# A decoder layer's quantized feed-forward: codes of x packed by the scalar engine and transposed by DMA instead of by TensorE, with the order of the down products changed

## What is computed

```
x = x + attention(layernorm(x))                 # 16 heads, window 128, 4 sinks
x = x + experts(layernorm(x), token ids, ctx)   # 4 experts, each token goes to one
x = x + ffn(layernorm(x))

def ffn(x):                                     # hidden size 2048
    h = silu(bit_linear(x, w_gate)) * bit_linear(x, w_up)
    h = ln_weight * h * rsqrt(mean(h * h) + 1e-6)
    return bit_linear(h, w_down)

def bit_linear(x, w):                           # activations to 8 bits per row, weights to -1, 0, 1
    s = 127 / clip(max(abs(x), axis=-1), 1e-5)
    q = clip(round(x * s), -128, 127) / s
    return q @ weight_quant(w).T
```

## Time and profile before

| | before |
|---|---|
| median of 3 runs | 798.23 us |
| lowest and highest | 793.23 and 798.83 us |
| the profiled execution's own time | 794.88 us |
| its span, from first to last instruction | 793.1 us |
| feed-forward, first gate product to the end | 588.5 to 793.1 us |
| mean granted TensorE clock | 0.987 of full speed |
| busy in the span | PE 92%, DVE 75%, ACT 60%, POOL 42% |

### The profile page before, as it was taken

How to read it: one execution, slowest core, us unless ns; L and a number is a source line. 1 busy time by engine, 2 the same in 40 slices (tenths; PEclk the granted TensorE clock), 3 DMA queues, 4 the chain that set the end, 5 groups by cost and what they waited for, 6 DMA issues and landing times. The chain is left out here.

```text
span 793.1 us, 14108 instructions
## 1 busy us (share of the span) xinstructions
PE 727.6 (92%) x5130; PEld 504.6 (64%) x5130; DVE 595.6 (75%) x1102; ACT 472.5 (60%) x1024; POOL 332.9 (42%) x330
## 2 busy tenths in 40 slices
PE   5988999999999999999987969999998989889894
PEld 4766777777777777777754658888873444334341
DVE  6886766886668856766676547788878999999972
ACT  4555766666667666766565224444447767766761
POOL 2011204213142134354374244445546667767661
PEclk9999999999999999999999989999999999999998
DMA  9300021304030331215330176555331223323231
GB/s 315 111 1 28 27 70 65 108 28 161 28 107 28 107 133 54 81 55 184 110 102 7 39 257 222 183 187 207 99 123 27 66 81 104 84 83 91 67 79 40
DMA packets 55218, 78.33 MB, mean 99 GB/s; under 512 B 36335, under 2 KB 38383, under 8 KB 53424
## 3 DMA queue, kind: packets, MB, share of 16 engines
q1 hardware_dynamic: 46336, 51.99, 20.7%
q0 software_dynamic: 8528, 24.93, 9.2%
q10 hardware_dynamic: 288, 0.52, 0.2%
HBM read 56.92 MB, written 17.59 MB: 94 GB/s over the span
## 5 line engine op out<-in xcount | busy, mean ns | idle before, releaser
L556 ACT ACTIVATE probs<-s_ps,neg_max 128x512 f32<-128x512 f32 (+2 forms) x256 | 152.5, 611 | 19.2 <-DVE neg_max L725 17.6
L725 DVE TENSOR_REDUCE neg_max<-s_ps 128x2 f32<-128x1024 f32 (+2 forms) x128 | 124.6, 1015 | 33.9 <-PE s_ps L963 33.4
L983 PE MATMUL pT_ps<-ident,probs 128*128 128x128 f32 x832 | 113.9, 277 | 11.0 <-DVE probs L746 9.7
L568 ACT ACTIVATE probs<-pT_ps 128x512 f32<-128x512 f32 x96 | 57.5, 599 | 98.6 <-PE pT_ps L983 97.7
L983 PEld LDWEIGHTS pT_ps<-ident,probs 128*128 128x128 f32 x832 | 92.6, 142 | 26.1 <-DVE probs L746 12.3
L746 DVE COPY probs<-pT_ps 128x512 f32<-128x512 f32 x112 | 76.7, 685 | 37.1 <-PE pT_ps L983 36.4
L1678 POOL TENSOR_TENSOR xg_own<-h,ln_w_sb 128x512 f32<-128x512 f32 x64 | 83.2, 1311 | 34.2 <-DVE h L1764 32.4
L896 PE MATMUL side_ps<-w_hi 128*128 128x512 f32 x172 | 71.1, 413 | 0.0
L420 POOL TENSOR_TENSOR aT_hi<-norm,one_col 128x512 fp32r<-128x512 f32 x15 | 15.6, 1042 | 125.6 <-DVE norm L737 87.4
L1867 PE MATMUL y_ps<-w_tern,hqT 128*128 128x512 bf16 x256 | 65.2, 379 | 2.8 <-DMA hqT<-hq 2.0
L896 PE MATMUL side_ps<-w_hi,w_lo 128*128 128x512 f32 x172 | 67.5, 392 | 0.0
(11 more groups left out here) (282 smaller groups left out, 1764.3 us busy)
## 6 DMA issues: line engine op xcount, KB each, us to landing
w_piece<-w_ffn SPq DMA_DIRECT2D x24, 512.0 KB
w_stage<-w_ffn SPq DMA_DIRECT2D x12, 1024.0 KB
xres<-x POOLq DMA_DIRECT2D x4, 1024.0 KB, 5.8
xn<-x SPq DMA_DIRECT2D x3, 1024.0 KB
x<-xres POOLq DMA_DIRECT2D x3, 1024.0 KB, 4.9
xn<-c SPq DMA_DIRECT2D x2, 1024.0 KB, 5.0
v_next<-c SPq DMA_DIRECT2D x2, 1024.0 KB, 7.8
xn<-x SPq DMA_DIRECT2D x4, 256.0 KB, 3.7
```

The source lines that it names most:

```text
L556: nc.scalar.activation(weights[qt][:, h, at:at + width(qt)], s_ps[:, h, 0:width(qt)], ACT.Exp, bias=neg_max[:, qt % 2, h:h + 1], accum_out ...
L568: nc.scalar.activation(out, turned_p, ACT.Identity).then_inc(slot_copied[0], 1)
L725: nc.vector.tensor_reduce(neg_max[:, qt % 2, 2 * s:2 * s + 2], s_ps[:, 2 * s:2 * s + 2, 0:width(qt)], AX.X, ALU.max, negate=True).then_inc ...
L983: last = nc.tensor.transpose(pT_ps[:, k % 2, h * P:h * P + P], weights[qt][:, h, a:z], ident[:])
```

## The change

- DVE no longer rounds x. ACT does, at the end of its tile behind gate 3, and then packs the codes of x to bf16 in a new tile `xq` (`quantize_x`, `pack_x`). SP issues a DMA transpose of them (`turn_x`). TensorE's transposes of x and ACT's copy out of PSUM are gone.
- The down products come one chunk later, one of them in the next tile; `y_of` stands behind hidden 0 of the next tile and is for tile t - 3; the store and the gather on POOL come one tile later.
- ACT does gate 2 ahead of both packings of h, not between them.
- DVE does hidden 1 ahead of the scale and the rounding of h, not behind them.
- `mean_of` is a tensor_scalar instead of a scalar_tensor_tensor.
- In the last expert tiles DVE does the clip ahead of the maximum of x; ACT rounds and packs x of tile 0 in the last but one expert tile and of tile 1 behind the last.
- `h_turned` is one semaphore for each half, so that the first two down quarters wait for the first half only.

```diff
+    def pack_x(self, act, t):
+        act.wait_ge(self.xq_ready, t + 1)
+        if t:
+            act.wait_ge(self.xqT_ready, t * 16)
+        self.nc.scalar.activation(self.xq[:], self.xq_code, ACT.Identity, bias=self.minus_offset[:]).then_inc(self.xq_packed, 1)
+
+    def turn_x(self, sp, t):
+        sp.wait_ge(self.xq_packed, t + 1)
+        self.nc.sync.dma_start_transpose(self.xqT[:, t % 2], self.xq[:]).then_inc(self.xqT_ready, 16)
...
-        self.nc.vector.scalar_tensor_tensor(self.mean_rstd[:, i:i + 1], self.bn_mv[:, i, 0:1], -1.0, self.rstd[:, i:i + 1],
-                                            ALU.mult, ALU.mult).then_inc(self.mean_ready, 1)
+        self.nc.vector.tensor_scalar(self.mean_rstd[:, i:i + 1], self.bn_mv[:, i, 0:1], self.rstd[:, i:i + 1], -1.0,
+                                     ALU.mult, ALU.mult).then_inc(self.mean_ready, 1)
...
-        self.nc.vector.tensor_scalar(self.xq_big[:], self.xn[:], self.x_inv[:], CODE, ALU.mult, ALU.add).then_inc(self.xq_ready, 1)
+        self.nc.scalar.activation(self.xq_big[:], self.xn[:], ACT.Identity, scale=self.x_inv[:], bias=self.code[:]).then_inc(self.xq_ready, 1)
...
@@ experts, scalar engine
-            if s == ROUTED_TILES - 1:
-                front.wait_scattered(act, 10)
-                act.wait_ge(front.consts, 4)
-                front.xqT_of(act, 0)
...
             if s == ROUTED_TILES - 2:
+                act.wait_ge(front.consts, 5)
+                front.wait_scattered(act, 9)
+                front.quantize_x(act, 0)
+                front.pack_x(act, 0)
                 front.normalize_x(act, 1)
+        front.quantize_x(act, 1)
+        front.pack_x(act, 1)
...
@@ feed-forward, SP
-        for t in range(TILES - 1):
-            turn(t)
+        front.turn_x(sp, 1)
+        for t in range(TILES):
+            if inside(t - 1):
+                turn(t - 1)
+            if inside(t + 2):
+                sp.wait_ge(up_summed, (t + 1) * FC)
+                front.turn_x(sp, t + 2)
...
@@ feed-forward, scalar engine
             gate_of(t, 1)
-            if inside(t + 1):
-                front.xqT_of(act, t + 1)
+            gate_of(t, 2)
             if inside(t - 1):
                 pack(t - 1, 0)
-            gate_of(t, 2)
             if inside(t - 1):
                 pack(t - 1, 1)
             gate_of(t, 3)
+            if inside(t + 2):
+                front.quantize_x(act, t + 2)
+                front.pack_x(act, t + 2)
             squares(t, 0)
...
@@ feed-forward, vector engine
+            if inside(t - LATE_DOWN - 1):
+                y_of(t - LATE_DOWN - 1)
             if inside(t - 1):
                 sum_squares(t - 1)
             if inside(t + 2):
                 front.top_of_x(dve, t + 2)
+            hidden(t, 1)
+            if inside(t + 2):
                 front.scale_x(dve, t + 2)
             if inside(t - 1):
                 scale_h(t - 1)
                 quantize_h(t - 1)
-            hidden(t, 1)
             hidden(t, 2)
-            if inside(t + 2):
-                front.quantize_x(dve, t + 2)
             if inside(t + 3):
                 front.stats_of(dve, t + 3)
                 front.variance_of(dve, t + 3)
             hidden(t, 3)
-            if inside(t - LATE_DOWN):
-                y_of(t - LATE_DOWN)
         last = TILES - 1
         top_of(last, 0)
+        y_of(last - LATE_DOWN)
         top_of(last, 1)
...
@@ feed-forward, TensorE
-                if c == 1 and t and inside(t + 1):
-                    front.transpose_x(pe, t + 1)
-                if inside(t - LATE_DOWN):
-                    down(t - LATE_DOWN, c)
+                quarter = (t - LATE_DOWN) * FC + c - 1
+                if quarter >= 0:
+                    down(quarter // FC, quarter % FC)
+        down(TILES - LATE_DOWN - 1, FC - 1)
```

More of the change, by code:

```diff
@@ L1137, in set_consts @@
         nc.gpsimd.memset(self.minus_offset[:], -CODE_ZERO).then_inc(self.consts, 1)
+        nc.gpsimd.memset(self.code[:], CODE).then_inc(self.consts, 1)
         nc.gpsimd.memset(self.ident[:], 0.0).then_inc(self.consts, 1)
-        pool.wait_ge(self.consts, 3)
+        pool.wait_ge(self.consts, 4)
         nc.gpsimd.affine_select(out=self.ident[:], in_=self.ident[:], compare_op=ALU.not_equal, fill=1.0, base=0,
@@ L1201, in scale_x @@
             dve.wait_ge(self.gu_ready, t)
+            dve.wait_ge(self.xq_ready, t)
         self.nc.vector.tensor_scalar(self.x_max127[:], self.x_max[:], Q_EPS, 1.0 / QMAX, ALU.max, ALU.mult).then_inc(self.xq_step, 1)
@@ L1204, in scale_x, with quantize_x @@
         self.nc.vector.reciprocal(self.x_inv[:], self.x_max127[:]).then_inc(self.xq_step, 1)
-    def quantize_x(self, dve, t):
-        dve.wait_ge(self.xq_step, (t + 1) * XQ_STEPS)
+    def quantize_x(self, act, t):
+        act.wait_ge(self.xq_step, (t + 1) * XQ_STEPS)
         if t:
-            dve.wait_ge(self.xq_transposed, t)
-        self.nc.vector.tensor_scalar(self.xq_big[:], self.xn[:], self.x_inv[:], CODE, ALU.mult, ALU.add).then_inc(self.xq_ready, 1)
[L1212 to L1218, removed]
+            act.wait_ge(self.xq_packed, t)
+        self.nc.scalar.activation(self.xq_big[:], self.xn[:], ACT.Identity, scale=self.x_inv[:], bias=self.code[:]).then_inc(self.xq_ready, 1)
 def expert_rows(sh, front):
@@ L1490, in vector_program @@
                 front.mean_of(dve, 1)
-            if s == last - 1:
+            if chunk_of(s) is not None:
+                clip(chunk_of(s))
+            if s == last - 2:
                 front.top_of_x(dve, 0)
                 front.scale_x(dve, 0)
[L1494 to L1498, removed]
         front.stats_of(dve, 2)
@@ L1549, in tensor_program @@
             if s == ROUTED_TILES - 1:
-                pe.wait_ge(front.consts, 4)
-                front.transpose_x(pe, 0)
+                pe.wait_ge(front.consts, 5)
             pe.wait_ge(a_ready, s + 1)
@@ L1618, in ffn_phase @@
     h_transposed, hqT_ready = sem("h_transposed"), sem("hqT_ready")
-    hq_packed, h_turned = sem("hq_packed"), sem("h_turned")
+    hq_packed, h_turned = sem("hq_packed"), [sem("h_turned0"), sem("h_turned1")]
     y_summed, y_ready = sem("y_summed"), sem("f_y_ready")
@@ L1637, in gate_up @@
         if c == 0:
-            pe.wait_ge(xqT_ready, t + 1)
+            pe.wait_ge(xqT_ready, (t + 1) * 16)
         if c >= 2 or inside(t - 1):
@@ L1648, in sync_program @@
     def sync_program(sp):
+        front.wait_scattered(sp, 10)
+        front.turn_x(sp, 0)
         sp.wait_ge(front.w_clipped, CHUNKS)
@@ L1658, in turn @@
                 sp.dma_start_transpose(hqT[:, t % 2, n * FK // HALVES:(n + 1) * FK // HALVES, :],
-                                       hq[:, n * HALF:n * HALF + HALF]).then_inc(h_turned, 16)
-        for t in range(TILES - 1):
-            turn(t)
+                                       hq[:, n * HALF:n * HALF + HALF]).then_inc(h_turned[n], 16)
+        front.turn_x(sp, 1)
[5 more added lines that the diff above has]
+                front.turn_x(sp, t + 2)
     def gpsimd_program(pool):
@@ L1699, in gpsimd_program @@
                 front.gu_scale_of(pool, t + 2)
-            if inside(t - LATE_DOWN):
-                store(t - LATE_DOWN)
-            if t >= LATE_DOWN + 1 and inside(t - LATE_DOWN - 1 + len(homes)):
-                front.gather(pool, t - LATE_DOWN - 1 + len(homes))
+            if inside(t - LATE_DOWN - 1):
+                store(t - LATE_DOWN - 1)
+            if t >= LATE_DOWN + 2 and inside(t - LATE_DOWN - 2 + len(homes)):
+                front.gather(pool, t - LATE_DOWN - 2 + len(homes))
         rms_of(TILES - 1)
-        for t in range(TILES - LATE_DOWN, TILES):
+        for t in range(TILES - LATE_DOWN - 1, TILES):
             store(t)
@@ L1719, in pack @@
             if inside(t - 1):
-                act.wait_ge(h_turned, t * HALVES * 16)
+                act.wait_ge(h_turned[n], t * 16)
             nc.scalar.activation(hq[:, cols], hq_code[:, cols], ACT.Identity, bias=minus_offset[:]).then_inc(hq_packed, 1)
@@ L1860, in down @@
             else:
-                pe.wait_ge(h_turned, (t + 1) * HALVES * 16)
+                pe.wait_ge(h_turned[g // HALVES], (t + 1) * 16)
             if g == 0 and inside(t - 1):
```

12 lines of the change are left out of this document (4 added, 8 removed).

## The result

| | before | after |
|---|---|---|
| median | 795.75 us (4 runs, 793.23 to 798.83) | 808.47 us (4 runs, 805.08 to 812.56) |
| profiled execution, its own time and span | 794.88, 793.1 us | 807.24, 805.5 us |
| mean granted TensorE clock | 0.987 | 0.982 |
| a feed-forward tile | 11.81 us | 12.48 us |

The ratio of the times is 1.0169, with a 95% interval of 1.0133 to 1.0204. The changed kernel is slower by 1.7%. I had said 804 us, 0.9% slower, and a tile of 12.34 us.

The account below looks back on a forecast made before the run. DVE was taken as fullest, but the new tile as bound by an ACT and DVE loop: 11.81 us plus 0.53 of POOL blocking. Terms - 0.9 + 1.7 + 5.9 + 0.2 = + 6.9 us; forecast 804 us, range 791 to 812.

Parts of the forecast that it names:

- same: Outcome for the whole kernel: a change within about 1%, 8 us; chance 0.52.
- slower: Outcome for the whole kernel: slower by more than about 1%, 8 us; chance 0.33.
- start, up to gate 3 of tile 0: Hand-over from the experts: first gate product no longer waits for TensorE's x transposes; 0.9 us less, bounds 0 and 1.3.
- tiles 3 to 13: Steady feed-forward tiles: 12.34 us each instead of 11.81, 5.9 us more over eleven.
- tiles 14 and 15: Last feed-forward tiles, without work for x: 11.06 and 10.3 us, together 0.2 us more.
- tail: From hidden 3 to the last store: the same up to 0.1 us.
- two squares of 1.05: ACT between gate 3 and gate 0: two squares of h, 1.05 us each, within the 4.11 us to gate 0.
- G + 4.05: When DVE alone would reach hidden 0, G being the start of gate 3; ACT puts it at G + 4.82.
- The lock: DVE's rounding of h held up by POOL's second weighting: first half 0.53 us late per tile, bounds 0 and 0.72.
- Rival A: Rounding not held up by POOL's weighting, or POOL misses it: tile 11.81 us, time unchanged, 795 to 798 us; chance 0.24.
- Rival C: TensorE's clock halves after its 2 us idle stretch: 2.7 us more a tile, 35 over 13; chance 0.09 with other slowdowns.
- 10.3 us of DVE work: DVE's tile without waits: 11.81 less 0.43 for rounding x, 0.60 for mean_of and 0.47 for gate 2.

Follow-up runs that it names:

- b3: Changed kernel with a separate output for each of the two squares of h, so the second needn't wait for the first; tile 12.27 us against 12.48.
- a1: Changed kernel with POOL's second weighting waiting until both halves of the rounding of h are done; median 801.65 us, ratio 1.0065 to the kernel before.
- a0: Changed kernel as it is, run again with the kernel before on another chip; ratio 1.0130, tiles of 12.48 us.
- d4: Changed kernel with second square behind gate 0, POOL's wait for both roundings, gate 3 ahead of the second packing, f_code 64 bytes wide; median 786.97 us.
- b4: Changed kernel with mean_of as a scalar_tensor_tensor again; one run 807.31 us, steady tile 12.48 us.
- b1: Changed kernel with second square of h behind gate 0 and POOL's second weighting behind both roundings; median 787.07 us, ratio 0.9893 to the kernel before.
- b5: Changed kernel with gate 2 between the two packings of h again; one run 813.9 us, tile 13.05 us.

## Why the prediction was right, and where its sum was off

The sign, the mechanism and the place are as forecast: ACT is what hidden 0 waits for, the rounding is held up by the weighting, and TensorE idles in one piece ahead of y_ps. The size is not. The measured median lies within the range, 4.5 us above the forecast and nearer to its edge than I should like. That the forecast came so near is luck in part: the 798.23 us that I built on came down to 795.75 with a fourth run, and from there the same sum gives 802.7. The 1.7% is beyond the 1% that I had allowed for "same", so of my three outcomes it is "slower", which had 0.33, and not the likelier "same". By spans the change is + 12.4 us, above even the + 3.5 to + 10.5 that I gave my own forecast, where the sum said + 6.9:

| term | forecast | measured |
|---|---|---|
| start, up to gate 3 of tile 0 | - 0.9 | + 1.2 |
| tiles 1 and 2 | + 1.7 | + 1.9 |
| tiles 3 to 13 | + 5.9 | + 7.7 |
| tiles 14 and 15 | + 0.2 | + 1.6 |
| tail | 0 | - 0.1 |

**The loop.** By the distances in the timeline after: gate 3 to gate 0 is 4.31 us (forecast 4.11), to hidden 0 0.70 (0.71), to the rounding 4.07 (4.1), to the packing 1.29 (0.79 + 0.53 = 1.32), two packings 2.10 (2.10). The sum is 12.47, and 12.48 is measured. quantize_x took 802 ns (forecast 802), pack_x 722 (690, between the bounds). The only term of size that was off is the pair of squares, "two squares of 1.05". In the tile that I read they stood apart, 1.41 us between their starts, the second waiting for h. Where nothing else holds the second, they are 1.22 apart, and b3 shows that the wait for the first is it. The trace of the kernel before had this too, in tile 14 (1.23 us, with no wait for h), which I had overlooked:

```profile
760.40 1.05 ACT L1736 ACTIVATE sq_junk<-h 128x1024 bf16<-128x1024 f32 x1
...
761.63 1.06 ACT L1736 ACTIVATE sq_junk<-h 128x1024 bf16<-128x1024 f32 x1
```

The tile is 0.14 us longer than forecast, which is 1.5 us of the missing 1.8 over eleven tiles; the other 0.3 is in one tile (the clock, below). Hidden 0 waits 0.96 us, where I had 0.8. DVE alone was ready for it at G + 4.05, as I said, though the terms I wrote for that add up to 3.92 only.

**The lock.** 0.53 us was forecast from one overlap in the rows, 0.52 was measured by a1. Rival A, no blocking, is out.

**The clock.** Rival C came true in one tile out of eleven, at 0.3 us where it had 2.7. Windows of the kernel after, and TensorE's timeline in the same stretch, which is in tile 3:

```profile
626.00:632.00 6.00, 3.25 (x11) 1.11 (x10) 4.84 (x15) 2.83 (x5) 2.68 (x3) 0.81 0.09 21
```

```profile
629.14 1.33 PE L1872 MATMUL y_ps<-w_tern,hqT 128*128 128x512 bf16 x4 [2.75 <-DVE xn L1811]
630.26 1.91 PE L1640 MATMUL e_xT_ps<-w_tern,xqT_home 128*128 128x512 bf16 x4
```

After an idle stretch of 2.75 us the granted clock is 0.81 in the mean of the six us, and a group of four matmuls takes 1.91 us instead of 1.03, as at 1.2 instead of 2.4 GHz. The granted clock is 0.50 up to about 633 and 1.00 from 634 on, so that some three groups were slow and not five. The tile is 12.77 us, 0.3 longer; the other stretches of 1.96 us a tile passed at 1.00 in this run. Not so in other runs. In a0 the clock fell to 0.50 twice behind an idle stretch of 1.96 to 1.97 us, in a tile of 12.77 among the eleven and in tile 14, which lasts 12.77 us there and 11.89 in the kernel after. The second of these, in a0:

```profile
767.70 1.02 PE L1872 MATMUL y_ps<-w_tern,hqT 128*128 128x512 bf16 x4 [1.96 <-DVE xn L1811]
768.56 1.81 PE L1640 MATMUL e_xT_ps<-w_tern,xqT_home 128*128 128x512 bf16 x4
```

b3 has no such tile among the eleven, 12.24 to 12.28 throughout, with idle stretches of 1.7 to 1.8 us and one of 2.55. So the length of the stretch alone doesn't tell when it comes; what else does stays open.

**Tiles 14 and 15.** I had 11.06 and 10.3 and measured 11.89 and 10.85. The failed step is "has 0.13 of blocking as before". Without the work for x in between, the rounding comes 0.93 us behind the start of the first weighting instead of 1.77, while that still runs, and both halves are caught (timeline of tile 14 after):

```profile
767.46 2.93 POOL L1682 TENSOR_TENSOR xg_own<-h,ln_w_sb 128x512 f32<-128x512 f32 x2
768.39 2.55 DVE L1806 TENSOR_SCALAR hq_big<-xg_own,h_mul 128x1024 f32<-128x1024 f32 x2
...
769.30 1.15 ACT L1725 ACTIVATE hq<-hq_big,minus_offset 128x1024 bf16<-128x1024 f16 x1
...
770.98 1.15 ACT L1725 ACTIVATE hq<-hq_big,minus_offset 128x1024 bf16<-128x1024 f16 x1 [0.53 <-DVE hq_big L1806]
```

The two weightings take 2.93 us instead of 2.48 and the two roundings 2.55 instead of 1.42: the engines take turns, weighting, rounding, weighting, rounding. One by one they take 1.25 us (from 767.46), 0.87 (768.39), 1.71 (768.68) and 1.76 (769.18). With POOL waiting (a1) these tiles are 11.26 and 10.48.

**The start.** From the transposes of expert tile 16 to gate 3 of tile 0 it is 22.37 us, 0.54 less than the 22.91 before; I had 0.9, and 0.54 is within my bounds. But the experts reach that point 1.78 us later, 16 times 0.09 of it from the longer expert tile. That was in no term of mine: I had taken the experts as untouched. What touched them is where the tensors behind f_code lie in SBUF, by d4.

**mean_of and the lighter DVE.** They brought nothing in the steady tiles, as forecast, since DVE waits for ACT. My reason for mean_of's 0.2 us, that the new form is free of POOL, holds where the two meet, but in the steady tiles the place alone would have freed it (b4). The 10.3 us of DVE work that I gave for a tile without waits is borne out as work, though no run reached it as a tile: in b1 DVE waits 0.50 us for gate 3 and 0.21 for POOL in 10.98, which leaves 10.27.

## What to carry to other kernels

Sum the work of each engine, but forecast from the loop that the in-order lists close from one tile to the next; making the fullest engine lighter by a tenth was worth nothing here, while another engine's list was what it waited for. Before adding to a list, look for what can stand behind the instruction that others wait for: one square moved by one line was worth 14 us, more than the whole change had cost. Where DVE and POOL can lock each other out, the time at which an input gets ready is part of the cost, and a wait added to the engine that has slack can pay.

## What the runs showed of the hardware that I had not expected

- The place of a tensor in SBUF changes matmul time. With an f_code of 4 or 8 bytes a row ahead of the later tensors, an expert tile, with its 24 fp32r matmuls, lasts 6.47 us; without it, or with 64 bytes, 6.37 to 6.38. The matmuls follow each other by 0.233 us instead of 0.229. Which operand it is, and whether 16 or 32 bytes would do, stays open.
- A second ACTIVATE with an accumulated output starts 1.22 us behind the first when it waits for the first's semaphore and 1.04 without the wait.
- When DVE and POOL both had a pair of instructions that lock each other out, they alternated; neither pair ran through (2.93 and 2.55 us in tile 14, against 2.48 in the steady tiles and 1.42 in a1).
- The clock fell after one idle stretch of 2.75 us in the kernel after and not after those of 1.96 in that run. In a0 it fell after two of 1.96 to 1.97, in b5 after two of 2.10 to 2.11; it did not after one of 2.55 in b3 or one of 2.89 in b5.
